# An eight-core attention and channel-mix layer: the load of the large weights moves into the attention, and the residual is no longer kept in DRAM

## The chip, the cores and the metric

The kernel runs as one program on the 8 cores of one Trainium2 chip. The cores don't talk to each other. The metric is device time in microseconds of the slowest core; lower is better. Each core has TensorE (PE), VectorE (DVE), ScalarE (ACT), GpSimd (POOL) and SyncE (SP). DMAs are issued here by SP, ACT and POOL; those that convert a type are issued by POOL.

## What is computed

x has the shape (4, 4096, 1024). With `ln` the layer norm over the last axis:

```python
h = ln(x); q, k, v = h @ Wq, h @ Wk, h @ Wv          # 64 columns each
att = softmax(einsum('bid,bkd->bik', q, k), axis=1)   # over the query index i
x = x + tile(att @ v, (1, 1, 16))                     # 64 columns repeated 16 times
z = ln(x); zp = z shifted down by one token (first row zero)
r = sigmoid((mu_r*z + (1-mu_r)*zp) @ W_r.T)
k = square(relu((mu_k*z + (1-mu_k)*zp) @ W_k.T))
x = x + r * (k @ W_v.T)
```

Core c takes batch c // 2 and half c % 2 of its 4096 tokens. It needs keys and values of all 4096 tokens, and gives the output of its own 2048 tokens (16 tiles of 128).

## The kernel before

The program is written out by hand, engine by engine. Each `@block.<engine>` function appends to that engine's queue in the order of the text, and a queue runs strictly in order; semaphores (`SV` counts DVE instructions, `SS` ACT's, `SM` PE's, and one or several per kind of DMA) set the rest. The stages carry letters in the names of their counters:

- **A, LayerNorm 1.** 32 tiles of 128 tokens. SP loads each tile of x into one of eight slots of `xst` (L279), DVE sums (L372), ACT squares (L306), DVE scales (L360) and POOL writes the bf16 result to `zdram` (L287). After every second group of four tiles ACT issues eight DMA transposes of that quarter into `zT` (L319).
- **Weights.** Behind its last `zdram` write POOL issues the three big loads `wrT`, `wkT`, `wvT` (L289 to L293): 4 MB of f32 each, converted to bf16. Nothing reads them before stage I.
- **C, q, k, v.** PE multiplies a quarter as soon as its transposes have landed (L397, L402), then v (L412); DVE evacuates.
- **D, attention.** The transposed v goes to `vdram` and comes back token-major by 32 small DMA transposes, issued one after the other by SP, each after the last has landed (L441, tile `v_sb`). For each of the 32 key tiles PE computes scores (L494), ACT takes the exponential of four pieces of 1024 queries (L554), DVE scales the key tile's v by the reciprocal of the sum (L532, needs its slice of `v_sb`), and PE accumulates (L475).
- **E, end of the attention.** PE and DVE bring the result into `out_tok` (128 x 16 x 64, f32, token-major), and SP makes three tiny DMAs one behind the other for the token before the core's own half (L614, L617, L619: `xrow_d`, `outx_row`, the row of x). DVE's first instruction of stage F (L704) waits for the last of them.
- **F, LayerNorm 2.** POOL loads the 16 own tiles of x again (L646), the first eight when stage E is done. DVE adds the attention result (`x1b`, L679), sums (L687) and later scales to `z1b` (L697). SP writes `x1b` to `x1dram` (L665) and `z1b` to `z1dram` (L668). ACT then issues two sets of eight transposes from `z1dram` to `z1T`: the low half (L770), and once all of these have landed the high half (L779), there one at a time.
- **H.** DVE mixes `z1T` with its shifted self into `xr` and `xk` (L809 to L821).
- **I, J.** PE multiplies by `wrT` (L842) with ACT's sigmoid into `r_sb` (L855), then by `wkT` (L884) with relu and square into `kaT`.
- **K.** For each of 16 tiles PE multiplies by `wvT` (L942). POOL reloads the tile of `x1dram` into `xst` (L961), DVE forms `tmp32 = ops * r_sb` (L988) and `x2b = tmp32 + xst` (L993), and SP writes `x2b` to `y_out` (L966). `x2b` and `tmp32` have two halves, so L988 of tile t also waits for the `y_out` write of tile t-2. PE has two PSUM tiles, freed by L988.

## Time and profile before

| | |
|---|---|
| time, median of 2 runs | 812.47 us (811.62 to 813.31) |
| the profiled execution | 815.21 us |
| span of its slowest core (core 7) | 813.2 us |
| spans of all cores | 796.3 to 813.2 us |
| busy time of core 7: PE, DVE, ACT | 353.8, 292.5, 244.0 us |
| DMA traffic of core 7 | 84.61 MB |

The profiled execution's time is 2.0 us more than the span of its slowest core. No engine is busy for half of the span: the stages have different limits, and in several of them every engine waits.

### The profile page before, as it was taken

How to read it: one execution, taken by the hardware profiler on the slowest of the kernel's cores; microseconds unless marked ns; L12 is line 12 of the kernel's file. 1: busy time of each engine (PE TensorE's matmuls, PEld its weight loads, DVE VectorE, ACT ScalarE, POOL GpSimd, SP SyncE). 2: the span in 40 equal slices, each digit the busy share in tenths (PEclk: the TensorE clock that was granted, in tenths of full speed). 3: DMA queues.
4: the chain of work that ended last, by engine and by line, in shares of the span. 5: the costliest groups of instructions: out<-in, count | busy, mean ns of one | idle time of the engine just before them, and what ended most of it. 6: DMA issues, size and time to landing. Idle time of an engine off the chain costs nothing.

```text
span 813.2 us, 5717 instructions; the slowest of 8 cores (796.3 to 813.2 us)
## 1 busy us (share of the span) xinstructions
PE 353.8 (44%) x1392; PEld 124.5 (15%) x1392; DVE 292.5 (36%) x515; ACT 244.0 (30%) x420; POOL 47.8 (6%) x77
## 2 busy tenths in 40 slices
PE   0004000007037788777775000000003699999995
PEld 0001000003013111111112000000001244444432
DVE  3541515247014111111113067661489200222665
ACT  2204013040000988888881032220000222432000
POOL 2111101131000000000001001100000000001110
PEclk9999555558569555666665555555557799999999
DMA  9666684949961000000001822669630000001885
GB/s 228 176 176 114 218 164 155 226 112 166 174 97 26 7 8 9 5 1 0 1 0 3 165 79 78 251 254 266 117 55 0 0 1 1 0 1 59 277 280 212
DMA packets 80158, 84.61 MB, mean 104 GB/s; under 512 B 60445, under 2 KB 60461, under 8 KB 80062
## 3 DMA queue, kind: packets, MB, share of 16 engines
q0 software_dynamic: 13504, 32.32, 16.6%
q1 hardware_dynamic: 14910, 39.07, 14.5%
q10 hardware_dynamic: 51712, 12.85, 10.4%
q8 instruction: 12, 0.20, 0.1%
q14 instruction: 20, 0.16, 0.1%
HBM read 47.79 MB, written 30.15 MB: 96 GB/s over the span
## 4 chain that ended last, share of the span: by engine, by line
PE 23%; DMA 23%; DVE 15%; issue 14%; ACTq 13%; ACT 9%; DVEq 1%; SPq 1%; POOL 1%; POOLq 0%
ACTq L319 10%; DMA xst<-x_in 8%; PE ktp L884 7%; ACT p_sb L554 7%; PE rps L842 6%; PE dpool L494 4%; DMA zdram<-zst 4%; DMA z1T<-z1dram 4%; DMA y_out<-x2b 3%; ACTq L770 3%; DVE xk L821 2%; PE ops L942 2%; DVE x1b L679 2%; DVE zst L360 2%; DMA outx_row<-xrow_d 2%
## 5 line engine op out<-in xcount | busy, mean ns | idle before, releaser
L554 ACT ACTIVATE p_sb<-dpool,negm 128x1024 bf16<-128x1024 f32 x128 | 140.6, 1124 | 22.2 <-DVE negm L519 20.8
L842 PE MATMUL rps<-wrT,xr 128*128 128x512 bf16 x256 | 58.9, 395 | 186.3 <-DVE xr L812 165.5
L494 PE MATMUL dpool<-qrep,krep 64*128 64x512 bf16 x256 | 102.0, 566 | 41.8 <-ACT p_sb L554 37.1
L397 PE MATMUL qk<-zT,wqk 128*128 128x512 bf16 x64 | 19.7, 465 | 211.7 <-DMA zT<-zdram 108.2
L306 ACT ACTIVATE junk<-xst 128x1024 bf16<-128x1024 f32 x32 | 33.8, 1057 | 87.1 <-issue 79.4
L842 PEld LDWEIGHTS rps<-wrT,xr 128*128 128x128 bf16 x256 | 25.7, 101 | 219.1 <-issue 191.2
L942 PE MATMUL ops<-wvT,kaT 128*128 128x512 bf16 x256 | 56.1, 379 | 6.0 <-DVE tmp L988 4.1
L372 DVE TENSOR_REDUCE sums<-xst 128x1 f32<-128x1024 f32 x32 | 39.0, 1220 | 51.1 <-DMA xst<-x_in 51.1
L884 PE MATMUL ktp<-xk,wkT 128*128 128x512 bf16 x256 | 55.6, 379 | 1.7 <-ACT r_sb L855 1.3
L525 DVE TENSOR_REDUCE ell<-ellp 128x1 f32<-128x4 f32 x32 | 5.0, 157 | 134.5 <-ACT p_sb L554 134.5
L909 DVE TENSOR_TENSOR kaT<-krl 128x512 bf16<-128x512 bf16 x32 | 13.6, 425 | 98.3 <-ACT krl L900 98.3
L397 PEld LDWEIGHTS qk<-zT,wqk 128*128 128x128 bf16 x64 | 7.0, 113 | 222.3 <-issue 217.6
L494 PEld LDWEIGHTS dpool<-qrep,krep 64*128 64x128 bf16 x256 | 16.5, 103 | 125.6 <-issue 125.3
L287 POOL DMA_DIRECT2D zdram<-zst x32 | 22.3, 704 | 154.1 <-DVE zst L360 154.1
L942 PEld LDWEIGHTS ops<-wvT,kaT 128*128 128x128 bf16 x256 | 24.7, 98 | 37.4 <-issue 8.6
L884 PEld LDWEIGHTS ktp<-xk,wkT 128*128 128x128 bf16 x256 | 24.9, 98 | 32.3 <-issue 2.6
L900 ACT ACTIVATE krl<-ktp 128x512 bf16<-128x512 f32 x32 | 19.0, 597 | 34.7 <-PE ktp L884 34.7
L646 POOL DMA_DIRECT2D xst<-x_in x16 | 9.7, 609 | 331.3 <-DVE outx_sb L608 259.0
L554 ACT ACTIVATION_READ_ACCUMULATOR p_sb<-dpool,negm 128x1 f32 x128 | 27.7, 217 | 0.0
L988 DVE TENSOR_TENSOR tmp<-ops,r_sb 128x1024 f32<-128x1024 f32 x16 | 19.6, 1224 | 22.4 <-DMA y_out<-x2b 15.5
L554 ACT ACT_TABLE_LOAD x1 | 1.3, 1283 | 86.6 <-DMA vdram<-p_sb 86.6
L855 ACT ACTIVATE r_sb<-rps 128x1024 bf16<-128x1024 f32 x16 | 16.3, 1024 | 36.6 <-PE rps L842 36.6
(82 smaller groups left out, 366.6 us busy)
## 6 DMA issues: line engine op xcount, KB each, us to landing
xst<-x_in SPq DMA_DIRECT2D x32, 512.0 KB, 8.1
zdram<-zst POOLq DMA_DIRECT2D x32, 256.0 KB, 8.1
xst<-x_in POOLq DMA_DIRECT2D x16, 512.0 KB, 14.4
x1dram<-x1b SPq DMA_DIRECT2D x16, 512.0 KB, 9.5
xst<-x1dram POOLq DMA_DIRECT2D x16, 512.0 KB, 6.2
y_out<-x2b SPq DMA_DIRECT2D x16, 512.0 KB, 4.7
z1dram<-z1b SPq DMA_DIRECT2D x16, 256.0 KB, 7.7
wrT<-wrT_in POOLq DMA_DIRECT2D x1, 2048.0 KB, 17.9
```

What stands on the lines that cost most here:

```text
L287: g.dma_start(out=zdram[i * 128:(i + 1) * 128, :], in_=zst[:, s * C:(s + 1) * C]).then_inc(ZAs[s], 16)
L306: sc.activation(junk[:, :], xst[:, (i % 8) * C:(i % 8 + 1) * C], AF.Square, accum_out=sumsq[:, i % 8:i % 8 + 1]).then_inc(SS, 1)
L319: sc.dma_start(out=zT[ctn][:, qtr * 1024:(qtr + 1) * 1024], in_=zdram[qtr * 1024:(qtr + 1) * 1024, ctn * 128:(ctn + 1) * 128], transpose=T ...
L372: v.reduce_sum(sums[:, i % 8:i % 8 + 1], xst[:, (i % 8) * C:(i % 8 + 1) * C], axis=AX.X).then_inc(SV, 1)
L397: t.matmul(qk[buf][:, :], wqk[:, ct * 128:(ct + 1) * 128], zT[ct][:, nch * 512:(nch + 1) * 512], start=(ct == 0), stop=(ct == CT - 1), ski ...
L494: t.matmul(units[u][:, cc * 512:(cc + 1) * 512], krep[64 * a:64 * (a + 1), kt * 128:(kt + 1) * 128], qrep[64 * a:64 * (a + 1), c * 512:(c ...
L554: sc.activation(p_sb[kt % 4][:, s * 1024:(s + 1) * 1024], units[u][:, :], AF.Exp, bias=negm[:, kt:kt + 1], accum_out=ellp[:, 4 * (kt % 2) + s:
L770: sc.dma_start(out=z1T[ctn][:, 0:1088], in_=z1dram[0:1088, ctn * 128:(ctn + 1) * 128], transpose=True).then_inc(SG_LO, 16)
L842: ins = t.matmul(r_ps[t_ % 2][:, hh * 512:(hh + 1) * 512], xr[ct][:, t_ * 128:(t_ + 1) * 128], wrT[:, ct * C + hh * 512:ct * C + (hh + 1) ...
L884: ins = t.matmul(kt_ps[ix % 2][:, :], wkT[:, ct * C + dt * 128:ct * C + (dt + 1) * 128], xk[ct][:, tc * 512:(tc + 1) * 512], start=(ct == ...
L942: ins = t.matmul(o_ps[t_ % 2][:, hh * 512:(hh + 1) * 512], kaT[dt][:, t_ * 128:(t_ + 1) * 128], wvT[:, dt * C + hh * 512:dt * C + (hh + 1) ...
L988: v.tensor_tensor(tmp32[:, (t_ % 2) * C:(t_ % 2 + 1) * C], o_ps[t_ % 2][:, :], r_sb[:, t_ * C:(t_ + 1) * C], ALU.mult).then_inc(SV, 1)
```

## The change

Four edits, which depend on each other in part.

1. POOL's three weight loads move out of stage A and stand behind the wait for the fourth exponential of key tile 7 (`d_exp(7, 3)`).
2. The first eight loads of x for stage F wait only for the last eight tiles of stage A (their slots of `xst`), not for the end of stage E. In POOL's queue they stand right behind the weight loads.
3. `x1b` is no longer written to `x1dram`; the DVE waits for these writes go.
4. Stage K loads the tile of x from the input again, and DVE adds the attention result a second time, by a third instruction on each tile. `out_tok` stays allocated until the end for that, so it moves down in the right-hand stack of SBUF.

```diff
-            g.dma_start(out=wrT[...], in_=wrT_in...).then_inc(SWB, 16)     # A, POOL
-            g.dma_start(out=wkT[...], in_=wkT_in...).then_inc(SWB, 16)
-            g.dma_start(out=wvT[...], in_=wvT_in...).then_inc(SWB, 16)
...
+        @block.gpsimd                                                      # D, POOL
+        def _(g):
+            g.wait_ge(SS, d_exp(7, 3))
+            g.dma_start(out=wrT[...], in_=wrT_in...).then_inc(SWB, 16)
+            g.dma_start(out=wkT[...], in_=wkT_in...).then_inc(SWB, 16)
+            g.dma_start(out=wvT[...], in_=wvT_in...).then_inc(SWB, 16)
...
                 else:                                                      # F, POOL, tiles 0 to 7
-                    g_.wait_ge(SV, SV_E)
-                    g_.wait_ge(SS, SS_D)
+                    g_.wait_ge(SV, A_CNT[("apply", 24 + t_)])
+                    g_.wait_ge(SS, a_square(24 + t_))
...
-                    sy.wait_ge(SV, F_CNT[("x1", t_)])                      # F, SP
-                    sy.dma_start(out=x1dram[t_ * 128:(t_ + 1) * 128, :],
-                                 in_=x1b[:, (t_ % 8) * C:(t_ % 8 + 1) * C]).then_inc(XSs[t_ % 8], 16)
...
-                    v.wait_ge(XSs[s8], xs_f(t_ - 8))                       # F, DVE, before x1b
...
-            for s in range(8):                                             # H, DVE, before mu1m
-                v.wait_ge(XSs[s], 32)
+            v.wait_ge(SS, f_square(15))
...
-                g.wait_ge(XSs[t_ % 8], xs_f(t_))                           # K, POOL
...
-                            in_=x1dram[t_ * 128:(t_ + 1) * 128, :]).then_inc(FSs[t_ % 8], 16)
+                            in_=x_in[t_ * 128:(t_ + 1) * 128, :]).then_inc(FSs[t_ % 8], 16)
...
+                v.wait_ge(SV, k_tmp(t_))                                   # K, DVE, after tmp32
+                v.tensor_tensor(tmp32[:, (t_ % 2) * C:(t_ % 2 + 1) * C],
+                                tmp32[:, (t_ % 2) * C:(t_ % 2 + 1) * C],
+                                bass.AP(out_tok, t_ * D, [[TOWN * D, 128], [0, 16], [1, D]]),
+                                ALU.add).then_inc(SV, 1)
                 v.wait_ge(FSs[t_ % 8], fs_k(t_))
-                v.wait_ge(SV, k_tmp(t_))
+                v.wait_ge(SV, k_mid(t_))
```

The first place is POOL's queue from the end of stage A to stage F. Before:

```order
L287 DMA zdram<-zst 128x1024 [waits SV] x32
L289 DMA wrT<-wrT_in 128x8x1024
L291 DMA wkT<-wkT_in 128x8x1024
L293 DMA wvT<-wvT_in 128x8x1024
L637 UNCONDITIONAL_BRANCH
L646 DMA xst<-x_in 128x1024 [waits SV,SS] x16
```

And with the change:

```order
L288 DMA zdram<-zst 128x1024 [waits SV] x32
L558 UNCONDITIONAL_BRANCH
L561 DMA wrT<-wrT_in 128x8x1024 [waits SS]
L563 DMA wkT<-wkT_in 128x8x1024
L565 DMA wvT<-wvT_in 128x8x1024
L645 UNCONDITIONAL_BRANCH
L654 DMA xst<-x_in 128x1024 [waits SV,SS] x16
```

The order is the same; what moved is the time at which the weights may go, by the wait on `SS` in front of `wrT`. The loads of x stay behind them.

The second place is SP's queue in stage F; `rowb` and `zst` give the rows of `z1dram` ahead of the own tokens and behind them, and the last two rows come 16 times, tile by tile. Before:

```order
L653 DMA z1dram<-rowb 1x1024 [waits SV,SD]
L656 DMA z1dram<-zst 63x1024 [waits SV,SD]
L659 DMA z1dram<-zst 64x1024 [waits SD]
L665 DMA x1dram<-x1b 128x1024 [waits SV]
L668 DMA z1dram<-z1b 128x1024 [waits SV]
```

And with the change:

```order
L661 DMA z1dram<-rowb 1x1024 [waits SV,SD]
L664 DMA z1dram<-zst 63x1024 [waits SV,SD]
L667 DMA z1dram<-zst 64x1024 [waits SD]
L673 DMA z1dram<-z1b 128x1024 [waits SV] x16
L970 UNCONDITIONAL_BRANCH
```

Sixteen of the 32 writes of this stage are gone from SP.

The third place is DVE's queue in stage K, tiles 0 to 2; `ops` is the PSUM tile, `YS` the semaphore of the `y_out` writes, `FS` that of the loads. Before:

```order
L988 TENSOR_TENSOR tmp32<-ops0,r_sb 128x1024 [waits SM,SS]
L993 TENSOR_TENSOR x2b<-tmp32,xst 128x1024 [waits FS0,SV]
L988 TENSOR_TENSOR tmp32<-ops1,r_sb 128x1024 [waits SM,SS]
L993 TENSOR_TENSOR x2b<-tmp32,xst 128x1024 [waits FS1,SV]
L988 TENSOR_TENSOR tmp32<-ops0,r_sb 128x1024 [waits SM,SS,SV,YS0]
L993 TENSOR_TENSOR x2b<-tmp32,xst 128x1024 [waits FS2,SV]
```

And with the change:

```order
L989 TENSOR_TENSOR tmp32<-ops0,r_sb 128x1024 [waits SM,SS]
L993 TENSOR_TENSOR tmp32<-tmp32,out_tok 128x1024 [waits SV]
L999 TENSOR_TENSOR x2b<-tmp32,xst 128x1024 [waits FS0,SV]
L989 TENSOR_TENSOR tmp32<-ops1,r_sb 128x1024 [waits SM,SS]
L993 TENSOR_TENSOR tmp32<-tmp32,out_tok 128x1024 [waits SV]
L999 TENSOR_TENSOR x2b<-tmp32,xst 128x1024 [waits FS1,SV]
L989 TENSOR_TENSOR tmp32<-ops0,r_sb 128x1024 [waits SM,SS,SV,YS0]
```

Between the product and the last sum of each tile stands one more instruction; the wait for the `y_out` write of two tiles before is still the first of the tile.

## Rows read from the trace of the kernel before

**Rows 1.** The view of the cores: span, mean granted clock.

```profile
core 6: 807.3 us, clock 0.696
core 7: 813.2 us, clock 0.710
```

**Rows 2.** Windows of core 7: PE, PEld, DVE, ACT, POOL busy; clock; DMA share; GB/s.

```profile
185.00:236.00 51.00, 14.86 (x63) 6.25 (x61) 12.83 (x19) 0.00 (x0) 0.10 (x1) 0.67 1.08 164
350.00:430.00 80.00, 60.76 (x188) 12.32 (x188) 12.24 (x75) 69.46 (x126) 0.00 (x0) 0.66 0.00 1
745.00:813.00 68.00, 56.33 (x258) 24.67 (x256) 39.45 (x33) 0.60 (x1) 8.45 (x16) 1.00 0.73 247
```

**Rows 3.** Timeline of core 7, 55 to 240 us: zT transposes, qk matmuls.

```profile
55.68 12.90 ACTq L319 DMA_TRANSPOSE zT<-zdram  x8
...
71.98 3.40 PE L397 MATMUL qk<-zT,wqk 128*128 128x512 bf16 x8 [71.98 <-DMA zT<-zdram]
...
185.16 47.51 ACTq L319 DMA_TRANSPOSE zT<-zdram  x8
...
197.97 1.89 PE L402 MATMUL qk<-zT,wkq 128*128 128x512 bf16 x8
...
236.04 3.29 PE L397 MATMUL qk<-zT,wqk 128*128 128x512 bf16 x8 [36.18 <-DMA zT<-zdram]
```

**Rows 4.** The DMA view of core 7: KB each, us from issue to landing.

```profile
wvT<-wvT_in POOLq DMA_DIRECT2D x1, 2048.0 KB, 44.3
```

**Rows 5.** The waits of core 6: us in total, times, longest.

```profile
PE qk L397 <- DMA zT<-zdram: 105.6, 2, 70.6
...
DVE rowf L704 <- DMA rowf<-x_in: 19.6, 1, 19.6
```

**Rows 6.** Tile v_sb of core 7: ns min/median/max, first and last start.

```profile
L441 SPq DMA_TRANSPOSE v_sb<-vdram x32: 1074/1075/1166, 264.1 to 337.1; - x32
```

**Rows 7.** Timeline of core 7's DVE, 268 to 310 us.

```profile
275.03 0.24 DVE L532 TENSOR_SCALAR vs_sb<-v_sb,rell 128x64 bf16<-128x64 bf16 x1 [0.18 <-DVE rell L529]
...
306.01 0.24 DVE L532 TENSOR_SCALAR vs_sb<-v_sb,rell 128x64 bf16<-128x64 bf16 x1 [0.18 <-DVE rell L529]
```

**Rows 8.** Chain of core 7 around 450 us: start, us, what.

```profile
443.58 6.91 DMA xrow_d<-outx_sb
450.55 12.37 DMA outx_row<-xrow_d
462.98 7.97 DMA rowf<-x_in
```

**Rows 9.** Timeline of core 7's DVE, LayerNorm 1, one group of four tiles.

```profile
76.23 2.98 DVE L360 TENSOR_SCALAR zst<-xst,srstd,snmr 128x1024 bf16<-128x1024 f32 x4
...
81.95 1.22 DVE L372 TENSOR_REDUCE sums<-xst 128x1 f32<-128x1024 f32 x1 [2.74 <-DMA xst<-x_in]
...
89.44 1.22 DVE L372 TENSOR_REDUCE sums<-xst 128x1 f32<-128x1024 f32 x1 [0.64 <-DMA xst<-x_in]
```

**Rows 10.** Timeline of core 7, 500 to 610 us: LayerNorm 2, z1T transposes.

```profile
500.77 2.98 DVE L697 TENSOR_SCALAR z1b<-x1b,srstd,snmr 128x1024 bf16<-128x1024 f32 x4
...
517.57 1.22 DVE L679 TENSOR_TENSOR x1b<-xst,out_tok 128x1024 f32<-128x1024 f32 x1
...
549.36 24.70 ACTq L770 DMA_TRANSPOSE z1T<-z1dram  x8
...
576.64 25.88 ACTq L779 DMA_TRANSPOSE z1T<-z1dram  x8
```

**Rows 11.** Tile x2b of core 7: ns min/median/max, first and last start; y_out landing.

```profile
L993 DVE TENSOR_TENSOR x2b<-tmp,xst x16: 1225/1226/1226, 752.2 to 809.0; 128x1024 f32<-128x1024 f32 x16
...
DMA to landing us min/median/max: 2.6/4.7/6.8
```

**Rows 12.** Tiles tmp and x1b of core 7: the first lines, same columns.

```profile
L988 DVE TENSOR_TENSOR tmp<-ops,r_sb x16: 1218/1225/1226, 750.9 to 807.7; 128x1024 f32<-128x1024 f32 x16
...
L679 DVE TENSOR_TENSOR x1b<-xst,out_tok x16: 1160/1217/1226, 479.3 to 539.1; 128x1024 f32<-128x1024 f32 x16
```

More of the change, by code:

```diff
@@ L253, in build_program @@
         k_mm = lambda t: SM_K0 + t + 1
-        k_tmp = lambda t: SV_K0 + 2 * t + 1
-        k_x2 = lambda t: SV_K0 + 2 * t + 2
+        k_tmp = lambda t: SV_K0 + 3 * t + 1
+        k_mid = lambda t: SV_K0 + 3 * t + 2
+        k_x2 = lambda t: SV_K0 + 3 * t + 3
         k_ydma = lambda t: 16 * (t + 1)
@@ L288, in _ @@
                             in_=zst[:, s * C:(s + 1) * C]).then_inc(ZAs[s], 16)
-            g.dma_start(out=wrT[:, :].rearrange("p (ct d) -> p ct d", d=C),
-                        in_=wrT_in.rearrange("(ct p) d -> p ct d", p=128)).then_inc(SWB, 16)
-            g.dma_start(out=wkT[:, :].rearrange("p (ct d) -> p ct d", d=C),
-                        in_=wkT_in.rearrange("(ct p) d -> p ct d", p=128)).then_inc(SWB, 16)
-            g.dma_start(out=wvT[:, :].rearrange("p (ct d) -> p ct d", d=C),
-                        in_=wvT_in.rearrange("(ct p) d -> p ct d", p=128)).then_inc(SWB, 16)
         @block.scalar
@@ L448, in build_program @@
         closes(cm_qk)
+        out_cm = [
+            nc.sbuf_tensor("out_tok", [128, TOWN * D], F32, side="right"),
+        ]
+        out_tok, = opens(out_cm)
         z1T_cm = [nc.sbuf_tensor(f"z1T{i}", [128, 2176], BF16, side="right") for i in range(CT)]
         z1T = opens(z1T_cm)
-        out_cm = [
+        out2_cm = [
             nc.sbuf_tensor("out_sb", [128, 1024], F32, side="right"),
-            nc.sbuf_tensor("out_tok", [128, TOWN * D], F32, side="right"),
             nc.sbuf_tensor("outx_sb", [64, 1], F32, side="right"),
@@ L456, in build_program @@
         ]
-        out_sb, out_tok, outx_sb, xp_sb = opens(out_cm)
+        out_sb, outx_sb, xp_sb = opens(out2_cm)
         cm_p23 = [nc.sbuf_tensor("p_sb2", [128, S], BF16, side="right"),
@@ L558, in _ @@
                                                      4 * (kt % 2) + s + 1]).then_inc(SS, 1)
+        @block.gpsimd
+        def _(g):
+            g.wait_ge(SS, d_exp(7, 3))
+            g.dma_start(out=wrT[:, :].rearrange("p (ct d) -> p ct d", d=C),
+                        in_=wrT_in.rearrange("(ct p) d -> p ct d", p=128)).then_inc(SWB, 16)
+            g.dma_start(out=wkT[:, :].rearrange("p (ct d) -> p ct d", d=C),
+                        in_=wkT_in.rearrange("(ct p) d -> p ct d", p=128)).then_inc(SWB, 16)
+            g.dma_start(out=wvT[:, :].rearrange("p (ct d) -> p ct d", d=C),
+                        in_=wvT_in.rearrange("(ct p) d -> p ct d", p=128)).then_inc(SWB, 16)
         @block.vector
@@ L787, in _ @@
                 g.dma_start(out=d_z1, in_=z1dram).then_inc(SW, 16)
-                g.dma_start(out=d_x1, in_=x1dram).then_inc(SW, 16)
-                g.wait_ge(SW, SW_SMALL + 176)
+                g.wait_ge(SW, SW_SMALL + 160)
         closes(x1f_cm)
-        closes(out_cm)
+        closes(out2_cm)
         xk_cm = [nc.sbuf_tensor(f"xk{i}", [128, 2048], BF16) for i in range(CT)]
@@ L1001, in build_program @@
         closes(r_sb_cm)
+        closes(out_cm)
     return nc
```

## The prediction

> **What bounds the kernel now.** I read the view of the cores first: core 7 ends last at 813.2 us, core 6 at 807.3 [rows 1]. No engine is busy through the span, so I went through the stages by windows and by the timeline, asking in each what ends the waits. Four places matter.
>
> The end of stage C: eight zT transposes that ACT issues at 185.16 take 47.51 us to issue, where the first quarter's eight took 12.90; the reader is to see that PE, which has finished its last ready product at 197.97 + 1.89 = 199.9, stands until 236.04 [rows 3]. The three weight loads were issued just before, and the last lands 44.3 us after its issue [rows 4]. In the window 185 to 236 the DMA engines are full [rows 2]: the transposes share them with weights that nobody needs before stage I.
>
> The end of stage E: three DMAs of a few bytes to 4 KB stand in the chain of waits with 6.91, 12.37 and 7.97 us [rows 8]. At the same moment POOL issues eight 512 KB loads of x. A DMA of 16 KB with no other traffic turns round in (337.1 - 264.1) / 31 = 2.35 us [rows 6].
>
> Stage F and the low transposes behind it: DVE waits for reloads of x behind each group of four tiles, and ACT's eight low transposes start at 549.36, take 24.70 us to issue, and the high ones start at 576.64 [rows 10]. SP writes x1dram through all of that.
>
> Stage K: PE needs 56.33 us for 258 matmuls, 3.5 us for the 16 of a tile, at the full clock, 1.00 [rows 2]. The starts of tmp go from 750.9 to 807.7, so a tile takes 56.8 / 15 = 3.79 us [rows 12]. What adds the 0.3 is the y_out write, which lands in 2.6 to 6.8 us, 4.7 in the middle [rows 11].
>
> The attention between them is bound by ACT: 69.46 us busy of 80, DMA share 0.00 [rows 2]. It has room for transfers.
>
> **The weights move.** Removed from stage C: the collision. The transposes then should need what the first quarter's needed, 12.90 us to issue and 71.98 - 55.68 - 12.90 = 3.4 us more until PE starts [rows 3]; that quarter too ran beside other traffic, so this is not the best case. They land at 185.16 + 12.9 + 3.4 = 201.5, and PE, free at 199.9, waits 1.6 us instead of 36.2. PE also loses the slow start: its eight matmuls at 236.04 take 3.29 us, those at 197.97 take 1.89 [rows 3], the two levels of 1.2 and 2.4 GHz, since it fell to the lower one while it stood idle. Together -36.2 + 1.6 - 1.4 = **-36.0 us** on core 7. Core 6 waits 70.6 of its 105.6 us for the earlier quarter, 35.0 here [rows 5]: -34.8. From below, no wait at all is 1.6 better; from above, if landing takes 2 us longer, 2 worse.
>
> Added to stage D: 12 MB of weights and behind them 4 MB of x, from the end of key tile 7 on. Alone the weights take at most the 44.3 us of [rows 4], since they had the transposes beside them there; x has a third of their bytes, some 15 us more: 60 us in all. What they can hurt is the v_sb chain on SP. The rows of the DVE view are its readings of slices 1 and 7, one every (306.01 - 275.03) / 6 = 5.16 us [rows 7]; the fourth exponential of key tile 7 ends just before the second. By then (306.0 - 264.1) / 2.35 = 17 slices have landed [rows 6], 0 to 16, so the first that may be missing, slice 17, is wanted ten readings later at 357.6, 52 us into the 60. Under load one small DMA took up to 12.37 us [rows 8]; at that price four more slices land within the 52 us, and slice 21 is wanted only 20 us after slice 17, when the loads are over. So I cost this at **0**, hidden by that lead of ten slices; if no slice at all landed under the load, it would be 60 - 52 = 8 us. POOL's issues come off no path: it has nothing else in its queue until stage F, and the loads of x now stand ready there, behind the weights. PE reads wrT only in stage I.
>
> **The early loads of x.** They land during the attention, so the three tiny DMAs of stage E run with no other traffic: 3 x 2.35 = 7.1 us instead of 27.5 [rows 6, 8], **-20.4 us** on core 7. Core 6 waits only 19.6 us there today [rows 5], 7.2 remain: **-12.4**. The nearest rows give at the one end 2.2 (the same chain less its hand-over), at the other some 3.3 each, halfway from 2.35 to the 4.7 of a 512 KB write [rows 11]; that is -13 to -9 on core 6. What is late next is the row arithmetic on DVE and ACT, which stays.
>
> The Trainium skill's page "DMA: Bandwidth & Descriptors", section "Anatomy of one DMA", gives a fixed cost of about 2.0 us plus bytes over 436 GB/s. By it the three would take 6 us, one less than by the row. By the same rule a 512 KB y_out write would land in an estimated 3.2 us, well under the 4.7 measured, and stage K below would cost 4 us instead of 9; I go by the rows.
>
> **No x1dram in stage F.** The first two groups have their x already. The other two reload: from the first scaling to the fourth x1b it takes 517.57 - 500.77 = 16.8 us [rows 10]. Stage A has the same loads and the same bf16 writes without an f32 write beside them; there the first reloaded tile is read 81.95 - 76.23 = 5.7 us after the first scaling and the fourth 13.2 us after it [rows 9]. In stage F DVE needs two instructions per tile, 1.22 us each and hand-over, 2.5 us, so its fourth x1b can start at 5.7 + 3 x 2.5 = 13.3. Saved: 3.5 us a group, twice, **-7 us**; at least half of it, if reloads come later than in stage A.
>
> **The low transposes.** Their 27.3 us from first issue to the start of the high ones become 12.9 + 3.4 as in stage A, a sixteenth more for 1088 rows instead of 1024: 17.3 us, **-10 us** [rows 3, 10]. Half of the writes beside them (z1dram) stay, hence -8 to -12. The high ones are issued one at a time with no traffic beside them, and don't change; DVE follows each. The wait of DVE for x1dram at the start of H ends before that and is worth nothing.
>
> **The third instruction in stage K.** It has L679's operands and its 1.22 us, 1.3 with the hand-over (L988's last start to L993's last start) [rows 11, 12]. DVE then needs 3 x 1.32 = 3.98 us a tile against PE's 3.5 and is the floor: 15 x (3.98 - 3.79) + 1.3 for the last tile = +4.2. But tile t also waits for the y_out write of t-2. A round of two tiles now is 2 x 3.79 = 7.58 us; one more instruction within the loop makes 8.9, 4.45 a tile, +9.9 and +1.3 = +11.2. Less traffic per microsecond shortens the writes, so I take 4.3 a tile, **+9 us**. If every write took the longest 6.8: (3.98 + 6.8) / 2 = 5.4 a tile, +25. Reading x from the input instead of x1dram is the same bytes: 0, and tiles wait for SV_J or a free slot as before.
>
> **Sum.** Core 7: 813.2 - 36.0 - 20.4 - 7 - 10 + 9 = 748.8. Core 6: 807.3 - 34.8 - 12.4 - 7 - 10 + 9 = 752.1, and it becomes the last. The profiled execution takes 2.0 us more than its span, 754.1; it is 2.7 above the median of the runs, so **751.4 us**, 7.5% less.
>
> **Rivals.**
> - *Stage K is dearer* (13%). For: the chain's y_out writes were long when reloads ran beside them, and every one of them is now on a loop that has grown. Against: the traffic per time falls. Price: +25 instead of +9, 767.
> - *The load isn't hidden in the attention* (5%). The v_sb chain stands still while weights and x pass, DVE holds up the next maximum and ACT with it. For: the queues share the DMA engines, as the transposes' 47.51 us against 12.90 show. Against: the lead. Price up to 8 us, 759; more if the transfer is slower than 60 us.
> - *Slower than before* (2%). The same mechanism at its worst: from the 52nd microsecond on each microsecond of load is one of the attention's. It outweighs the gain of 61 us only if the loads last over 113 us; at 120 us the time is 820. They took 44 us for three quarters of the bytes, in worse company.
> - *PE's clock falls in stage K* (4%). PE would wait for DVE on every tile, busy 3.5 of 4.3 us. For: in the attention it is busy 60.76 of 80 us and is granted 0.66 [rows 2]. At 1.2 GHz a tile costs 7 us of PE, and 16 of them 112 instead of 61: some +45 net, 797. Against: in the window of stage K PE already waits, is busy 56.33 of 68 us, and is granted 1.00 with all 128 rows in use.
> - *The small DMAs or the transposes stay slow for a reason of their own* (6%): then 12 us of E or 10 of the low transposes don't come, 762. That the weights were not what slowed stage C, so that 36 us stay, I hold for nearly excluded by the quarter that took 12.90.
>
> The clock's rival rests on a rule of the Trainium skill too: "TensorE: Matmul & The Clock Gate", section "A second HAM failure mode", says that PE may swing between both levels when it idles briefly between groups for its PSUM tiles. The trace has such waits in stage K at clock 1.00, so I give it little.
>
> **How the numbers follow.** 70% for the forecast, whose own range is 741 to 760: its low end takes the good ends at once, 807.3 - 36.4 - 13 - 7 - 12 + 4.2 = 743 and 0.7 off, a little wider for the cores' scatter. The range that should hold 8 in 10 reaches over the dearer stage K: 740 to 770. About 2% is what a measurement of this kernel can tell from no change, 796 to 829. Faster by more: 0.95; within it 0.03 (the clock's case at its worst); slower 0.02.
>
> **What would show it.** Right: the last quarter's zT transposes issue in about 13 us and PE's wait in front of them nearly gone; v_sb's last issue later than 73 us after its first, with no wait of vs_sb for it; three DMAs of 2 to 3 us in stage E; a tmp every 4.3 us and DVE nearly always busy in stage K. Wrong: vs_sb or the exponentials waiting during the weights; tmp waiting for y_out by more than 16 us in sum; a clock below 1.00 in stage K. The likeliest fault in size is the step of stage K, the next the E chain on the core that ends last.

## The result and the profile after

| | before | changed |
|---|---|---|
| median | 814.9 us (10 runs, 811.62 to 833.57) | 760.47 us (11 runs, 756.84 to 787.2) |
| profiled execution | 815.21 us | 762.89 us |
| span of the slowest core | 813.2 us (core 7) | 761.3 us (core 3) |

The ratio is 0.933, 95% interval 0.929 to 0.937: 6.7% faster, where 7.5% were forecast (751.4 us, range 740 to 770). The 814.9 us are also 2.4 above the 812.47 that the forecast started from. The median of before beside a kernel, here and below, comes from runs on the same chip. Some runs have one die disturbed; the medians and ranges are of all runs, the ratios leave those out.

The view of the cores of the changed kernel, as in [rows 1]:

```profile
core 3: 761.3 us, clock 0.725
...
core 6: 748.9 us, clock 0.715
core 7: 754.8 us, clock 0.711
```

Core 7 no longer ends last, and neither does core 6: core 3 does. So I compare the stages over all eight cores. Each number below is a difference of first starts of one instruction each, read from the tile views of a core (first start of the `vdram` write, of `out_sb`, `xrow_d`, `rowf`, and so on), and the mean over the 8 cores of the profiled execution.

| stretch, us | before | changed | difference |
|---|---|---|---|
| start to the write of `vdram` (A to C) | 258.8 | 221.0 | -37.8 |
| to the copy `out_sb` (D, attention) | 172.1 | 172.1 | 0 |
| to the issue of `xrow_d` (PE and DVE in E) | 11.5 | 11.5 | 0 |
| to the first `rowf` sum on DVE (three small DMAs) | 22.1 | 12.1 | -10.0 |
| to the first `x1b` | 8.3 | 8.3 | 0 |
| to the last `x1b` (F) | 60.3 | 56.3 | -4.0 |
| to the low z1T transposes | 10.3 | 10.3 | 0 |
| to the high ones | 26.0 | 17.6 | -8.4 |
| to K's first `tmp` (H, I, J) | 174.1 | 173.3 | -0.8 |
| first to last `tmp` (K) | 56.4 | 65.0 | +8.6 |
| last `tmp` to the last `x2b` | 1.3 | 2.7 | +1.4 |
| start of the last `x2b` | 801.1 | 750.1 | -51.0 |

**Stage C.** The timeline of core 7, as in [rows 3]; behind the duration stands the engine, in the brackets how long it stood before and for whom:

```profile
153.32 11.35 ACTq L314 DMA_TRANSPOSE zT<-zdram  x8
...
184.46 3.57 PE L392 MATMUL qk<-zT,wqk 128*128 128x512 bf16 x8 [105.67 <-DVE qrep L423]
...
185.27 11.72 ACTq L314 DMA_TRANSPOSE zT<-zdram  x8
...
190.27 1.89 PE L392 MATMUL qk<-zT,wqk 128*128 128x512 bf16 x8
...
205.81 1.89 PE L397 MATMUL qk<-zT,wkq 128*128 128x512 bf16 x8
```

The last quarter's eight transposes issue in 11.72 us instead of 47.51, as fast as those of the quarter before (11.35). PE takes the last three quarters in one go, twelve groups of eight matmuls from 184.46 on. The first two groups, behind a long wait, take 3.57 and 2.61 us; the ten from 190.27 on take 1.89 each, as at the higher clock level in [rows 3], and no wait stands in front of the last quarter's four. The 36.18 us wait is gone, and with it the second fall to the lower clock level. PE's one long wait here is that of 105.67 us ahead of the second quarter. The kernel before has it too (103.57 us); by the row it ended with an evacuation by DVE, which is at work on LayerNorm 1 until then. So of the second and third quarter it is not true, in either kernel, that PE multiplies them as soon as they have landed.

**Stage D.** The timeline of core 7, POOL's issues of the first weight and of x:

```profile
269.04 0.90 POOL L561 DMA_DIRECT2D wrT<-wrT_in  x1 [86.30 <-ACT p_sb L552]
...
271.68 4.27 POOL L654 DMA_DIRECT2D xst<-x_in  x8
```

The tile view of `v_sb` on core 7, as in [rows 6]:

```profile
L436 SPq DMA_TRANSPOSE v_sb<-vdram x32: 1074/1076/1520, 227.3 to 336.7; - x32
...
its engine sat idle before it (us, times) until:
...
  DMA v_sb<-vdram: 0.5, 3
...
DMA to landing us min/median/max: 2.2/2.2/7.5
```

The loads go out behind key tile 7: the first weight at 269.04, the first x at 271.68. The chain of 32 small transposes now takes 336.7 - 227.3 = 109.4 us instead of 73.0, since single ones take up to 7.5 us to land; DVE waits for it 0.5 us in all. The last of the eight x tiles lands at 323.7, so the load lasts 54.7 us; every slice from slice 16 on (the first is 0) still lands 37.5 us or more ahead of its reader. The stage lasts 172.1 us before and after.

**Stage E.** The chain that ended last on core 7, as in [rows 8] (start, us, what):

```profile
406.24 6.94 DMA xrow_d<-outx_sb
...
413.24 2.11 DMA outx_row<-xrow_d
...
415.41 1.51 DMA rowf<-x_in
```

The same on core 3, which ends last:

```profile
408.10 8.42 DMA xrow_d<-outx_sb
...
416.59 1.78 DMA outx_row<-xrow_d
...
418.43 1.41 DMA rowf<-x_in
```

The first, 64 pieces of 4 bytes from 64 partitions to DRAM, takes 6.94 and 8.42 us, and 7.2 on the mean of the eight cores. The second and third take 1.4 to 2.1 us on these two cores; over all eight they take 1.4 to 3.4, on average 2.5 and 2.3, so these two are as forecast.

**Stage F and the low transposes.** The timeline of core 7, one group of stage F, as in [rows 10]:

```profile
446.75 2.98 DVE L701 TENSOR_SCALAR z1b<-x1b,srstd,snmr 128x1024 bf16<-128x1024 f32 x4
...
448.18 2.71 POOL L654 DMA_DIRECT2D xst<-x_in  x4 [172.24 <-DVE z1b L701]
...
454.77 1.23 DVE L683 TENSOR_TENSOR x1b<-xst,out_tok 128x1024 f32<-128x1024 f32 x1 [5.03 <-DMA xst<-x_in]
...
462.35 1.22 DVE L683 TENSOR_TENSOR x1b<-xst,out_tok 128x1024 f32<-128x1024 f32 x1
```

And ACT's issues of the z1T transposes behind it:

```profile
492.02 14.46 ACTq L774 DMA_TRANSPOSE z1T<-z1dram  x8
...
509.37 25.68 ACTq L783 DMA_TRANSPOSE z1T<-z1dram  x8
```

From the first scaling to the fourth `x1b` it takes 462.35 - 446.75 = 15.6 us, where 16.8 stood before and 13.3 were forecast: the reload lands 454.77 - 448.18 = 6.6 us after its issue, and the first reloaded tile comes 8.0 us after the first scaling instead of the 5.7 of [rows 9]. The low transposes take 509.37 - 492.02 = 17.35 us to the high ones, where 17.3 was the forecast.

**Stage K.** The tile view of `tmp` on core 7, as in [rows 12]:

```profile
L989 DVE TENSOR_TENSOR tmp<-ops,r_sb x16: 1217/1218/1225, 683.8 to 747.9; 128x1024 f32<-128x1024 f32 x16
...
its engine sat idle before it (us, times) until:
  DMA y_out<-x2b: 6.9, 4
```

The tile view of `x2b` there, for the landing of `y_out`, as in [rows 11]:

```profile
DMA to landing us min/median/max: 2.6/3.3/6.3
```

DVE's timeline on core 7 over a tile that waited and one that didn't:

```profile
720.51 1.23 DVE L989 TENSOR_TENSOR tmp<-ops,r_sb 128x1024 f32<-128x1024 f32 x1 [2.48 <-DMA y_out<-x2b]
...
723.17 1.23 DVE L999 TENSOR_TENSOR x2b<-tmp,xst 128x1024 f32<-128x1024 f32 x1
724.31 1.22 DVE L989 TENSOR_TENSOR tmp<-ops,r_sb 128x1024 f32<-128x1024 f32 x1
...
728.10 1.22 DVE L989 TENSOR_TENSOR tmp<-ops,r_sb 128x1024 f32<-128x1024 f32 x1
```

The window of stage K on core 7, with the columns of [rows 2], and a short one inside it:

```profile
680.00:750.00 70.00, 58.35 (x256) 24.73 (x256) 56.16 (x47) 0.00 (x0) 8.44 (x16) 0.97 0.70 232
...
705.00:710.00 5.00, 2.07 (x6) 0.86 (x7) 3.24 (x3) 0.00 (x0) 0.00 (x0) 0.81 0.67 197
```

PE's timeline in the same stage:

```profile
679.97 20.88 PE L944 MATMUL ops<-wvT,kaT 128*128 128x512 bf16 x96 [1.81 <-DVE kaT L911]
...
707.93 12.21 PE L944 MATMUL ops<-wvT,kaT 128*128 128x512 bf16 x48 [3.29 <-DVE tmp L989]
```

A tile without a wait takes 728.10 - 724.31 = 3.79 us; that at 720.51 had to wait 2.48 us for the `y_out` write of two tiles before. Only four tiles wait so, 6.9 us in all (5.5 to 10.1 on the eight cores), and (747.9 - 683.8) / 15 = 4.27 us a tile comes of it. In the kernel before, the same view has more of these waits:

```profile
  DMA y_out<-x2b: 15.5, 9
```

The third instruction adds 15 x 1.33 = 20 us of work to DVE and only 7.3 us to the stage on core 7 (64.1 for 56.8). Of the rest, 8.6 us stood before as waits for writes (15.5 less 6.9) and 2.7 as waits for PE (6.7 less 4.0).

PE runs through its first six tiles and then waits for DVE eight times. The granted clock is 0.97, so PE is nearly all the time at the higher of its levels (over the stage 0.95 to 1.00 on the eight cores). It dips to 0.81 in the short window, where PE stands 3.29 us for a DVE that stands for `y_out`. The dip costs nothing: DVE waits for PE once in the stage, 4.0 us at the first tile, on every core.

### The profile page after: what moved, and what is told of

Same layout as the page of the kernel before. It is cut to its first block, busy times and chain, and to the rows that moved or that the text cites. A ratio compares the mean times of both kernels' runs of the same rounds, so it can differ in the third digit from the quotient of the medians.

```text
span 761.3 us, 5687 instructions; the slowest of 8 cores (748.9 to 761.3 us)
## 1 busy us (share of the span) xinstructions
PE 352.5 (46%) x1392; PEld 124.3 (16%) x1392; DVE 310.9 (41%) x531; ACT 243.9 (32%) x420; POOL 47.7 (6%) x77
## 3 DMA queue, kind: packets, MB, share of 16 engines
q10 hardware_dynamic: 51712, 12.85, 10.6%
## 4 chain that ended last, share of the span: by engine, by line
PE 26%; DMA 21%; DVE 18%; issue 15%; ACT 10%; ACTq 7%; DVEq 1%; SPq 1%; POOL 0%; POOLq 0%
DMA xst<-x_in 8%; PE ktp L886 7%; ACT p_sb L552 7%; PE rps L844 7%; PE dpool L492 5%; ACTq L314 5%; DMA zdram<-zst 4%; DMA z1T<-z1dram 4%; DMA y_out<-x2b 3%; DVE x1b L683 3%; DVE xk L823 2%; ACTq L774 2%; DVE tmp L993 2%; DVE tmp L989 2%; DVE zst L355 2%
## 5 line engine op out<-in xcount | busy, mean ns | idle before, releaser
L492 PE MATMUL dpool<-qrep,krep 64*128 64x512 bf16 x256 | 99.9, 558 | 43.7 <-ACT p_sb L552 39.2
L392 PE MATMUL qk<-zT,wqk 128*128 128x512 bf16 x64 | 17.8, 428 | 178.6 <-DVE qrep L423 107.7
L944 PE MATMUL ops<-wvT,kaT 128*128 128x512 bf16 x256 | 58.5, 387 | 10.4 <-DVE tmp L989 8.6
L844 PEld LDWEIGHTS rps<-wrT,xr 128*128 128x128 bf16 x256 | 25.9, 102 | 192.1 <-issue 164.6
L944 PEld LDWEIGHTS ops<-wvT,kaT 128*128 128x128 bf16 x256 | 24.8, 99 | 44.2 <-issue 17.3
L473 PE MATMUL dpool<-p_sb,vs_sb 128*64 128x512 bf16 x112 | 26.9, 634 | 0.0
## 6 DMA issues: line engine op xcount, KB each, us to landing
wrT<-wrT_in POOLq DMA_DIRECT2D x1, 2048.0 KB, 17.3
```

What stands on the lines that cost most here:

```text
L392: t.matmul(qk[buf][:, :], wqk[:, ct * 128:(ct + 1) * 128], zT[ct][:, nch * 512:(nch + 1) * 512], start=(ct == 0), stop=(ct == CT - 1), ski ...
L473: t.matmul(dpool[64 * half:64 * half + 64, (w % 2) * 512:(w % 2) * 512 + 512], vs_sb[:, tt_ * D:(tt_ + 1) * D], p_sb[tt_ % 4][:, w * 512:( ...
L492: t.matmul(units[u][:, cc * 512:(cc + 1) * 512], krep[64 * a:64 * (a + 1), kt * 128:(kt + 1) * 128], qrep[64 * a:64 * (a + 1), c * 512:(c ...
L844: ins = t.matmul(r_ps[t_ % 2][:, hh * 512:(hh + 1) * 512], xr[ct][:, t_ * 128:(t_ + 1) * 128], wrT[:, ct * C + hh * 512:ct * C + (hh + 1) ...
L944: ins = t.matmul(o_ps[t_ % 2][:, hh * 512:(hh + 1) * 512], kaT[dt][:, t_ * 128:(t_ + 1) * 128], wvT[:, dt * C + hh * 512:dt * C + (hh + 1) ...
```

## The experiments

Each diff is against the changed kernel or, for the first four, against the kernel before. Stage times are means over the 8 cores as in the table. The theory is that the four edits act in places of their own, by the sums of the prediction.

**e1_weights_only.** The kernel before with edit 1 alone.

```diff
-            g.dma_start(out=wrT[...], ...)       # POOL, end of A (wkT, wvT too)
+        @block.gpsimd
+        def _(g):
+            g.wait_ge(SS, d_exp(7, 3))
+            g.dma_start(out=wrT[...], ...)       # wkT, wvT too
```

> Edit 1 alone: the three weight loads go behind the fourth exponential of key tile 7, everything else as before. My theory: stage C loses its wait, the start of the attention comes 36 to 38 us earlier on every core, the attention keeps its 172 us and all later stages keep theirs, so the ratio to before is about 0.954. Rival (the load is only moved, the attention pays): stage C gains the same, but the attention gets longer by 8 us or more and the ratio is 0.965 or higher.

Measured: ratio 0.950 (0.942 to 0.958), 775.03 us against 812.94. The stretch to `vdram` is 218.9 us, 39.9 less than before; stage D 172.2; the E chain (22.6), F (60.4) and the low transposes (26.5) are as before. The row of core 7's timeline:

```profile
182.84 11.99 ACTq L313 DMA_TRANSPOSE zT<-zdram  x8
```

So one edit brings most of the gain (5.0% of the 6.7%), and by taking the load away from the transposes.

**e2_early_x_only.** The kernel before with edit 2 alone.

```diff
                 else:
-                    g_.wait_ge(SV, SV_E)
-                    g_.wait_ge(SS, SS_D)
+                    g_.wait_ge(SV, A_CNT[("apply", 24 + t_)])
+                    g_.wait_ge(SS, a_square(24 + t_))
```

> Edit 2 alone: the first eight loads of x for LayerNorm 2 stand right behind the weights, which still go at the end of stage A. My theory: 4 MB more stand in the traffic beside the last eight transposes, so PE's wait there grows from 36 us by up to 15; stage E shortens from 22 us to about 12 on the mean of the cores. Net between 5 us faster and 5 us slower, ratio 0.994 to 1.006. Rival: x behind the weights doesn't reach the transposes, which are through by then; then only the 10 us of stage E show, ratio 0.988.

Measured: ratio 1.001 (0.998 to 1.005), 813.34 us against 812.94, no change. The E chain falls from 22.1 to 12.7 us, and the stretch to `vdram` grows from 258.8 to 269.7. The timeline of core 7 shows where the gain is lost:

```profile
186.37 59.34 ACTq L319 DMA_TRANSPOSE zT<-zdram  x8
...
248.49 3.49 PE L397 MATMUL qk<-zT,wqk 128*128 128x512 bf16 x8 [46.74 <-DMA zT<-zdram]
```

With the weights still in stage A, the eight loads of x follow them into the same window: the transposes need 59.34 us to issue instead of 47.51, and PE waits 46.74 instead of 36.18. The edit's 9.4 us remain only behind the first one (e4). It is e1 from the other side: 4 MB more beside the transposes cost some 11 us.

**e3_no_x1dram_only.** The kernel before with edits 3 and 4 (`x1dram` gone, three instructions a tile in K).

```diff
-                    sy.dma_start(out=x1dram[...], in_=x1b[...])      # F, SP
...
-                            in_=x1dram[t_ * 128:(t_ + 1) * 128, :])  # K, POOL
+                            in_=x_in[t_ * 128:(t_ + 1) * 128, :])
...
+                v.tensor_tensor(tmp32, tmp32, <out_tok repeated 16 times>, ALU.add)
```

> Edits 3 and 4 alone: no write of x1dram, x read again in stage K and a third DVE instruction there. My theory: stage F 4 us shorter, the low transposes 8 to 10 us shorter, stage K 10 us longer, sum -2 to -4 us, ratio 0.995 to 0.998. Rival: the low transposes are slowed by the z1dram writes and not by x1dram, then they gain under 3 us and the kernel is 3 us or more slower, ratio 1.004.

Measured: ratio 0.994 (0.991 to 0.998), 807.38 us. F is 3.3 us shorter, the low transposes 8.6, K 4.7 and the last tile 1.3 longer. The gains in F and in the transposes stand here without the others, so they belong to the missing writes. K costs less here than in the changed kernel, which is taken up below.

**e4_weights_and_early_x.** Edits 1 and 2 together, the rest as before.

> Edits 1 and 2: weights in the attention, the first eight x behind them; x1dram and stage K as before. My theory: 37 us from stage C and about 10 us from stage E on the mean core, ratio about 0.943; the three tiny DMAs of stage E take as long as in the changed kernel, about 12 us in sum, with the first at 8 us. Rival: the first tiny DMA was slow in the changed kernel by chance of its neighbours; then it takes 2 to 3 us here and the ratio is 0.937.

Measured: ratio 0.937 (0.930 to 0.944), 762.47 us, which is the changed kernel's time within the intervals. The stretch to `vdram` is 218.8 us as in e1, and the E chain 12.3 instead of e1's 22.6: behind edit 1, edit 2 keeps its gain. Edits 3 and 4 add nothing to these two that could be measured: in the changed kernel their -4.0 and -8.4 stand against +8.6 and +1.4. The chain of core 7 shows the first small DMA as slow as in the changed kernel:

```profile
396.77 6.92 DMA xrow_d<-outx_sb
```

**e5_four_x2b.** The changed kernel with four halves of `x2b` and a semaphore each, so that a tile waits for the `y_out` write of four tiles before.

```diff
-                v.wait_ge(YSs[t_ % 2], ys_k(t_ - 2))                 # t_ >= 2
+                v.wait_ge(XSs[t_ % 4], 16 * (t_ // 4))               # t_ >= 4
...
-                v.tensor_tensor(x2b[:, (t_ % 2) * C:(t_ % 2 + 1) * C],
+                v.tensor_tensor(x2b[:, (t_ % 4) * C:(t_ % 4 + 1) * C],
```

> The changed kernel with four halves of x2b instead of two, so that a tile in stage K waits for the y_out write of four tiles before. My theory: DVE's three instructions set the floor of 3.79 us a tile and the waits for y_out add the rest (65.0 us for 15 tiles on the mean of the cores); with the waits gone stage K takes 57 to 59 us, the kernel 6 to 8 us less, ratio to before about 0.925. Rival: the reloads of x are late as well and take the place of the y_out waits; then stage K stays above 62 us and the ratio at 0.931 or more.

Measured: ratio 0.934 (0.925 to 0.942), 762.43 us, from runs between 753.04 and 794.11. The interval holds the changed kernel's 0.933 as well as the 0.925 that was expected, so the time of the whole kernel settles nothing. The stage does. From the first to the last `tmp` it takes 57.2 or 57.3 us on every one of the eight cores, against 63.0 to 67.5; the tile view of core 7:

```profile
L990 DVE TENSOR_TENSOR tmp<-ops,r_sb x16: 1216/1218/1224, 680.2 to 737.5; 128x1024 f32<-128x1024 f32 x16
...
  PE ops L944: 4.0, 1
```

No wait for `y_out` is left, and 57.3 / 15 = 3.82 us is what three instructions cost DVE. So of the +8.6 us of stage K 0.9 is the longer floor (57.3 against 56.4, which had its own waits in it) and 7.7 the wait for the write of two tiles before.

**e6_row_in_sbuf.** The changed kernel with the attention row of the token before computed as one row, with `xp_sb` as the weights and `vs_sb` moving, and copied to `outx_row` by DVE; the row of x is loaded at the start of stage D. The two other small DMAs are gone.

```diff
-                t.matmul(ox_e[:, 0:1], vs_sb[...], xp_sb[:, kt:kt + 1],
+                t.matmul(ox_e[0:1, 0:D], xp_sb[:, kt:kt + 1], vs_sb[...],
...
-            v.tensor_copy(outx_sb[:, :], ox_e[:, 0:1])
+            v.tensor_copy(outx_row[:, :], ox_e[0:1, 0:D])
```

> The changed kernel with the attention row of the token before formed as a row (operands of the 32 small products exchanged), copied by DVE straight to its place, and the row of x loaded at the start of the attention: no DMA is left in stage E. My theory: the 12.1 us from the first tiny DMA to DVE's first instruction of stage F fall to under 1 us, the kernel 11 us less, ratio 0.920. Rival: something else is late there next (ACT's table load, the zeroed rows), and at least 4 us of the 11 stay, ratio 0.925 or more.

Measured: ratio 0.922 (0.917 to 0.926), 747.04 us. DVE's timeline on core 7:

```profile
404.72 0.21 DVE L617 COPY outx_row<-oxe 1x64 f32<-1x64 f32 x1 [1.92 <-PE oxe L604]
405.04 1.22 DVE L700 TENSOR_TENSOR rowf<-rowf,outx_row 1x1024 f32<-1x1024 f32 x1
```

The copy ends at 404.93 and the sum starts at 405.04: 12.1 us have become 0.1. Nothing else in the stage wanted the time, so the chain stood whole on the path: the last `x2b` starts 14.0 us earlier than in the changed kernel on the mean of the cores, 12.0 from here and 3.0 from a shorter stage K, less 1.0 elsewhere.

**e7_weights_at_once.** The changed kernel with the loads sent at the start of stage D, without a lead of key tiles.

```diff
-            g.wait_ge(SS, d_exp(7, 3))
+            g.wait_ge(SV, SV_C)
```

> The changed kernel with the weights let go at the start of the attention instead of behind key tile 7: the lead of the v_sb chain is taken away. In the changed kernel the chain's 31 steps take 110 us instead of 73, so 37 us are lost while 16 MB pass; a slice then comes every 6 to 7 us and DVE wants one every 5.2. My theory: without the lead DVE waits for v_sb by 8 to 16 us in sum in the first 60 us of the attention, stage D grows from 172 to 180 to 188 us and the ratio to before is 0.943 to 0.953. Rival (the lead isn't needed, the attention's own slack hides the chain): stage D stays below 175 us and the ratio at 0.933.

Measured: ratio 0.951 (0.945 to 0.958), 771.35 us. Stage D takes 183.5 us instead of 172.1. The longest wait in DVE's timeline on core 7, and the sum in the tile view of `v_sb` there:

```profile
246.20 0.24 DVE L530 TENSOR_SCALAR vs_sb<-v_sb,rell 128x64 bf16<-128x64 bf16 x1 [4.41 <-DMA v_sb<-vdram]
```

```profile
its engine sat idle before it (us, times) until:
  DMA v_sb<-vdram: 10.5, 4
```

Four readings of `v_sb` wait 10.5 us on core 7, and its stage D is 10.6 longer (182.5 for 171.9); over the eight cores the waits are 10.5 to 13.7 us and the stage is 11.4 longer on average. A wait here goes whole into the attention. It is the rival "the load isn't hidden in the attention", produced by taking the lead away, and it shows that the lead hid it.

**e8_row_through_dram.** The changed kernel with the row as in e6 but still by way of DRAM: one piece of 256 bytes in place of 64 pieces of 4 bytes, and the three DMAs one behind the other as before.

```diff
-            sy.dma_start(out=xrow_d.rearrange("a (p o) -> p (a o)", p=64),
-                         in_=outx_sb[0:64, 0:1]).then_inc(SD, 16)
+            sy.dma_start(out=xrow_d, in_=outx_sb[:, :]).then_inc(SD, 16)
```

> The changed kernel with the attention row of the token before formed as a row, but still written to DRAM and read back; the write is one piece of 256 bytes from one partition instead of 64 pieces of 4 bytes from 64 partitions. My theory: the pieces of 4 bytes are what makes the first tiny DMA take 6.5 to 8.4 us beside 1.4 to 3 us for the other two; it falls to about 2 us, stage E's three DMAs to 6 to 7 us, the kernel 5 us less, ratio 0.927. Rival: the first DMA is slow since it is the first behind a long rest of the queue; then it stays at 6 us or more and the ratio at 0.933.

Measured: ratio 0.929 (0.923 to 0.934), 752.72 us. The chain of core 7:

```profile
405.07 1.17 DMA xrow_d<-outx_sb
...
406.30 1.19 DMA outx_row<-xrow_d
...
407.56 1.53 DMA rowf<-x_in
```

The same 256 bytes to the same place take 1.17 us instead of 6.94 (core 3: 1.19 instead of 8.42), and the chain 3.9 instead of 12.1 on average. The form of the first transfer made it slow, not other traffic; whether the 4-byte pieces or the 64 partitions do it, this run doesn't separate. Of the 8.2 us saved on average the first DMA gave 6.0. The two behind it have the same form as before and got faster too, from 2.5 to 1.2 us and from 2.3 to 1.4; why, no run here shows. By the time of the whole kernel alone this run can't be told from the changed kernel (0.933), whose interval overlaps.

The Trainium skill's page "DMA: Bandwidth & Descriptors", section "Rules for kernel authors", leaves open, for a load, whether the same bytes go faster to one partition or spread over many; here, for a write, one is faster, 1.17 against 6.94 us. Its section "Anatomy of one DMA" gives GpSimd's DMAs a fixed cost of about 2.0 us; these three, issued by SP, take 1.17, 1.19 and 1.53. So the 6 us that the prediction worked out by it for three DMAs of SP fit neither the 12.1 of the changed kernel nor the 3.9 here.

**e9_early_reload.** The changed kernel with the reload of stage F waiting for the `x1b` sum that last read its slot, not for the scaling four tiles later; `x1b` then waits for the scaling.

```diff
-                    g_.wait_ge(SV, F_CNT[("apply", t_ - 8)])         # F, POOL
-                    g_.wait_ge(SS, f_square(t_ - 8))
+                    g_.wait_ge(SV, F_CNT[("x1", t_ - 8)])
...
                 if t_ >= 8:                                          # F, DVE
+                    v.wait_ge(SV, F_CNT[("apply", t_ - 8)])
```

> The changed kernel with one wait loosened: the second eight loads of x for LayerNorm 2 wait for the x1b sum that reads their slot of xst, not for the scaling of that tile. My theory: the 8 to 11 us that DVE still waits for these loads in stage F are all their late start; stage F (first to last x1b) falls from 56.3 to 47 to 49 us, ratio to before 0.923. Rival: the loads then stand beside nothing but SP's writes and land as late as before since the z1dram writes take the DMA engines; then at least 4 us of the waits stay and the ratio is 0.929 or more.

Measured: ratio 0.920 (0.915 to 0.925), 748.73 us. F takes 46.8 us instead of 56.3. The tile view of `x1b` in the changed kernel, core 7:

```profile
L683 DVE TENSOR_TENSOR x1b<-xst,out_tok x16: 1160/1216/1227, 425.3 to 481.7; 128x1024 f32<-128x1024 f32 x16
...
its engine sat idle before it (us, times) until:
...
  DMA xst<-x_in: 9.1, 2
```

The same view of this one:

```profile
L683 DVE TENSOR_TENSOR x1b<-xst,out_tok x16: 1160/1215/1219, 424.2 to 471.0; 128x1024 f32<-128x1024 f32 x16
```

The last `x1b` starts 46.8 us after the first instead of 56.4. Of the 9.6 us saved 9.1 stood as "DMA xst" in the changed kernel. A slot of `xst` is free as soon as `x1b` has been formed from it, so these waits can be removed outright.

**e10_residual_ready.** The changed kernel with the attention result added to x before stage K: for 14 tiles DVE does it in stages I and J, in space that is free by then (`xst`, `wrT`, `zst`), for two in K; and with the four halves of e5.

```diff
+        @block.vector                                                # before stage I
+        def _(v):
+            for t_ in range(8):
+                x1_add(v, t_)                  # x of tile t_ + out_tok, in place
...
+                    if ix >= 12 and ix % 3 == 0 and ix < 30:         # J
+                        x1_add(v, 8 + (ix - 12) // 3)
...
-                v.tensor_tensor(tmp32, tmp32, <out_tok repeated 16 times>, ALU.add)
+                if t_ >= 14:                                         # K
+                    x1_add(v, t_)
```

> The changed kernel with four halves of x2b, and the residual of 14 of the 16 tiles made ready before stage K: x is loaded behind the last transposes (eight tiles into xst, four into the space of wrT when stage I is over, two into zst), and DVE adds the attention result in place while it is idle in stages I and J. Stage K has two DVE instructions a tile again, three for the last two tiles, and hardly any loads. My theory: stage K becomes PE's, 3.52 us a tile, 53 to 54 us for 15 tiles against 65 in the changed kernel, the last step 1.3 instead of 2.7; about 13 us less, ratio 0.917; stages H to J keep their times. Rival: the loads in H and the adds in J hold up the transposes, the products or the squares, and 5 us or more come back there, ratio 0.923 or more.

Measured: ratio 0.924 (0.919 to 0.929), 751.67 us. The expected 0.917 lies outside that interval. In the profiled execution the last `x2b` starts 11.8 us earlier than in the changed kernel on the mean of the cores, where 13 were expected. K takes 52.2 us; stages H to J 0.8 us more. The tile view of core 7:

```profile
L1018 DVE TENSOR_TENSOR tmp<-ops,r_sb x16: 1217/1225/1225, 680.2 to 732.4; 128x1024 f32<-128x1024 f32 x16
...
  PE ops L984: 16.8, 15
```

Now PE is what each tile waits for, 15 times, and 52.2 / 15 = 3.48 us a tile is its time for 16 matmuls, the 3.5 of [rows 2].

**e11_all.** e6, e9 and e10 together.

> The two before this one and the row without DRAM together: no DMA in stage E, second reload of stage F early, residual ready before stage K, four halves of x2b. My theory: the parts lie in different stages and add up: 11 or 12 from E, 8 from F, 13 from K, some 32 us below the changed kernel, ratio to before 0.893 to 0.900. Rival: with x reloaded earlier something else ends last in stage F (ACT's squares, the z1dram writes), and the sum is 5 us or more short, ratio above 0.902.

Measured: ratio 0.896 (0.891 to 0.901), 729.25 us (727.67 to 729.84), 4% less than the changed kernel and the fastest of all. The stages carry over: 46.8 in F, 17.5 for the low transposes, 52.2 in K. The core that ends last:

```profile
core 7: 727.4 us, clock 0.725
```

## Why the prediction was nearly right

The direction, most of the reasons and the range held; the forecast was 9.1 us low, 2.4 of them because the kernel before came out at 814.9 and not 812.47. Core by core it held less well: core 6 was to end last at 752.1 and ended first at 748.9, core 7 took 754.8 for 748.8, and the last is core 3, for which no sum was made. By its own steps:

- **The weights move: right.** -36.0 and -34.8 were forecast for cores 7 and 6, the mean is -37.8, core 7's -36.8, and core 3's, which ends last now, is 260.4 - 224.4 = -36.0. On core 6 it is -48.6 (265.0 to 216.4), more than its 35.0 us wait. The mark differs by several us from core to core, 216.4 to 225.1 in the changed kernel, and no run here was made for that. That core 6 came out near its 752.1 is luck: these 13.8 us too many cover what the other steps lack. e1 shows the gain by itself.
- **Its cost in stage D at 0: right, by the reason given.** The stage takes 172.1 us before and after, and e7 shows the 11.4 us that are due without the lead. The load lasted 54.7 us on core 7 where 60 were taken. The lead was larger than it had to be: 37.5 us of it were left at the tightest slice of the loaded stretch, since most of the slow DMAs took about 7 us and not the 12.37 that were taken, so some seven slices landed in that time and not four.
- **The early loads of x: mis-sized.** "The three tiny DMAs of stage E run with no other traffic: 3 x 2.35 = 7.1 us" is the step that failed. They took 12.1 on average: core 7 gained 16.7 for 20.4, core 6 gained 7.5 for 12.4, outside the stated bounds of -13 to -9 on that core (halfway from 2.35 to 4.7 is 3.5 a DMA and not 3.3; the -9 goes by 3.5). The second and third took 2.5 and 2.3 us on average, as forecast; the first took 7.2 in place of 2.35, which is nearly all of the difference. It was not like the row it was costed by, a transpose of 16 KB, since it has 64 pieces of 4 bytes (e8). [rows 8] showed the three only under load, where the first, 6.91, was the shortest. On core 7 that was nearly all its own, 6.94 without the load; on average it was 8.2 with the load and 7.2 without. On the core that ends last the term gave only 19.2 - 11.8 = 7.4.
- **No x1dram in stage F: right in kind, half in size.** -4.0 for -7; the stated lower bound was half. The first reloaded tile comes 8.0 us after the first scaling and not the 5.7 that were taken from stage A, where SP loads. Whether POOL's issue or other traffic makes the 2.3 us wasn't tried. e3 shows the gain, e9 the wait that was left.
- **The low transposes: right.** 17.6 us for 17.3. The gain is -8.4 and not -10 since before they took 26.0 on average, and 27.3 on core 7, from which the term was taken.
- **The third instruction in stage K: right in size, half wrong in its make-up.** +9 was forecast, +8.6 and +1.4 measured. The floor of 3.98 us a tile (3 x 1.32 is 3.96) was too high: the first instruction of a tile follows the last of the tile before after 1.14 us (723.17 to 724.31), not 1.32, so it is 3.79 to 3.82. And "4.3 a tile" comes from a few late writes of 5.5 to 10.1 us in sum, not from each. "DVE nearly always busy" is right between them. The bounds +4.2 and +25 held.
- **The rivals.** The attention hid the load; neither of the two slow outcomes came. "A clock below 1.00 in stage K" was named as a sign of being wrong, and it did show, 0.97 on core 7, but DVE's wait for PE stayed at 4.0 us, so nothing of the +45 came. "The small DMAs stay slow for a reason of their own", 6%, is in part what happened: one of three did. Its price, 762, lies near the 760.47 measured by luck: it stood for 12 us of E or 10 of the transposes, and of E 3.7 us were missing on core 7 and 4.9 on core 6.

The sum for core 3, which the prediction didn't make, would have been 807.0 - 36.0 - 12.1 - 7 - 10 + 9 = 750.9; it measured 761.3. Of the 10.4 us the E chain gave 4.7, F 3.6, the low transposes 2.4 (25.9 to 18.3) and K 1.5 (+9.2 and +1.3), together 12.2, and the other stages took 1.8 off. Costing only cores 6 and 7 was itself a weakness: the spans of the changed kernel lie within 12.4 us of each other, and 4 us more on one core make it the last.

**What stays open.** Stage K of the same code takes 61.1 us in e3, 62.0 in e6 and e7, 64.0 in e9, 64.4 in e8 and 65.0 in the changed kernel, nearly all of the difference in waits for `y_out`; e5 shows 57.3 without them. What makes single writes later in one kernel than in another is not shown. The reloads of x run beside the writes, and that how the two fall together makes it is a guess that no run here tests.

## What to carry to other kernels

Before a load is moved into "free" time, count the slices that are ready ahead of their readers where it starts: here ten of them made 16 MB free, and none made it cost 11 us (e7). An edit that sends a load earlier was worth nothing here as long as the window it landed in was full (e2: -9.4 and +10.9). Take the price of a DMA from a row with the same layout, not the same bytes; and when a buffer's reuse is what an engine waits for, look which of its readers the wait names: one written for the wrong one cost 9.5 us here (e9).

## What the runs showed of the hardware

- 256 bytes from 64 partitions, 4 bytes each, took 6.55 to 8.42 us to DRAM on the eight cores of the changed kernel, and 6.78 to 10.53 beside the loads of x in the kernel before; as one piece from one partition they took 1.12 to 1.19 (e8).
- On DVE in stage K an instruction that waits for the result of the one before it starts 1.32 to 1.33 us after it, one that doesn't after 1.14, before the 1.225 us of the last are over.
- Beside 16 MB of loads by POOL, 9 to 11 of the 32 small DMA transposes of 16 KB took over 3 us to land, up to 8.0 instead of 2.2, and the chain of 32 grew by half (105 to 110 us instead of 71 to 73).
